# One layer of a vision tower on one core: the front of the kernel rebuilt around a convolution read from PSUM, and the skip term moved to VectorE

## What is computed

```python
h = patches @ proj_w.T + proj_b + pos_emb                 # 1024 tokens x 192
xz = layernorm(h) @ in_proj_w.T                           # 384 channels x, 384 channels gate
x = silu(causal_conv(x, conv_w, K=4) + conv_b)            # per channel, along the 64 tokens of an image
ts, Bm, Cm = split(x @ x_proj_w.T, [48, 64])              # 48, 16, 16
dt = softplus(ts @ dt_proj_w.T + dt_proj_b)               # last token of an image: dt *= alpha
state = exp(A * dt) * state + dt * Bm * x                 # scan along the tokens, 384 x 16 states
y = (sum_n(state * Cm) + x * D) * silu(gate)              # last token: y *= feature_gating
h = h + y @ out_proj_w.T
h = h + shared_ffn(layernorm(h)) + sum of the top 2 of 8 experts, by token
```

## Time and profile before

| | us |
|---|---|
| median of 3 runs | 408.27 (407.31 to 408.51) |
| the profiled execution, its own time | 407.58 |
| its span | 405.5 |
| TensorE busy | 361.1 (89%) |
| VectorE busy | 223.4 (55%) |
| ScalarE busy | 214.6 (53%) |
| GpSimd busy | 218.6 (54%) |

### The profile page before, as it was taken

The page is one execution under the profiler, slowest core; times in us unless marked ns, Lnnn a source line. Parts: engine busy times, 40 slices in busy tenths (PEclk is TensorE's granted clock), DMA queues, the critical chain, the costliest instruction groups (busy, mean ns, idle before and its releaser), DMA issues.

```text
span 405.5 us, 5557 instructions
## 1 busy us (share of the span) xinstructions
PE 361.1 (89%) x1686; PEld 256.8 (63%) x1687; DVE 223.4 (55%) x327; ACT 214.6 (53%) x388; POOL 218.6 (54%) x160
## 2 busy tenths in 40 slices
PE   4798959898997799999999997999999999999970
PEld 3642224554564455566657775778888888888860
DVE  0467849856596284687897466874433232233220
ACT  0045789917599598397458645862333333333310
POOL 2110478967689486488999923770033333443333
PEclk9999969999999899999999958999999999999996
DMA  7950540000004341201059999225223322223211
GB/s 207 309 179 0 224 194 0 0 6 0 2 0 157 154 166 42 78 2 52 2 162 216 240 215 229 82 93 108 66 39 53 60 46 45 45 45 47 40 19 19
DMA packets 28595, 36.95 MB, mean 91 GB/s; under 512 B 6064, under 2 KB 24032, under 8 KB 27552
## 3 DMA queue, kind: packets, MB, share of 16 engines
q1 hardware_dynamic: 18768, 27.38, 24.1%
q0 software_dynamic: 4080, 4.39, 7.0%
q10 hardware_dynamic: 5728, 4.93, 4.3%
HBM read 28.29 MB, written 8.40 MB: 90 GB/s over the span
## 4 chain that ended last, share of the span: by engine, by line
PE 41%; DMA 21%; ACT 12%; DVE 10%; issue 7%; ACTq 5%; POOLq 1%; POOL 1%; SPq 1%; DVEq 0%
DMA out<-ysb,token_r 18%; PE ps L1326 11%; PE ps L1343 5%; ACT decays L710 4%; ACT diagB L698 4%; DVE states L962 4%; PE ps L1481 3%; DMA w_raw<-in_w13T 3%; PE ps L1238 2%; PE ps L1236 2%; ACTq L647 2%; DVE ysb L1142 2%; PE ps L1448 2%; PE ps L1268 1%; PE ps L1247 1%
## 5 line engine op out<-in xcount | busy, mean ns | idle before, releaser
L521 POOL TENSOR_TENSOR states<-states,c_all 128x1024 f32<-128x1024 f32 x48 | 114.2, 2388 | 35.8 <-DVE states L962 35.4
L962 DVE TENSOR_TENSOR_SCAN states<-decays,ps 128x1024 f32<-128x1024 f32 x48 | 109.1, 2282 | 43.8 <-PE ps L1326 34.7
L1326 PE MATMUL ps<-diagB,dt_uT 128*128 128x512 f32 x192 | 94.1, 615 | 1.9 <-ACT dt_uT L688 1.0
L602 POOL DMA_INDIRECT out<-ysb,token_r x23 | 36.1, 1571 | 68.1 <-DVE ysb L1142 62.8
L710 ACT ACTIVATE decays<-dt_uT,negA 128x504 f32<-128x504 f32 x96 | 60.4, 706 | 18.4 <-DVE states L962 18.4
L1343 PEld LDWEIGHTS ps<-ident,states 128*128 128x128 f32 x384 | 44.9, 141 | 22.5 <-issue 21.8
L1326 PEld LDWEIGHTS ps<-diagB,dt_uT 128*128 128x128 f32 x192 | 34.0, 197 | 32.5 <-issue 27.5
L1131 DVE TENSOR_TENSOR hm<-ps,sa 128x512 f32<-128x512 f32 x31 | 21.4, 691 | 55.3 <-PE ps L1454 53.9
L1343 PE MATMUL ps<-ident,states 128*128 128x128 f32 x384 | 49.7, 273 | 0.1
L812 ACT ACTIVATE sa<-ps 128x512 f32<-128x512 f32 x31 | 18.5, 598 | 55.2 <-PE ps L1454 53.8
L1481 PE MATMUL ps<-w,hT 128*128 (+1 forms) x248 | 45.5, 327 | 0.1
(11 more groups left out here) (177 smaller groups left out, 513.7 us busy)
## 6 DMA issues: line engine op xcount, KB each, us to landing
c_all<-c_scratch SPq DMA_DIRECT2D x8, 1024.0 KB, 4.8
w_raw<-in_w13T SPq DMA_DIRECT2D x9, 512.0 KB, 12.6
w_raw<-in_w13T SPq DMA_DIRECT2D x18, 256.0 KB, 12.3
w<-in_w2T SPq DMA_DIRECT2D x9, 384.0 KB, 3.5
xs<-rows_scratch SPq DMA_DIRECT2D x23, 128.0 KB, 2.3
rows_scratch<-dt_uT ACTq DMA_DIRECT2D x5, 520.0 KB, 8.5
c_all<-in_xT SPq DMA_DIRECT2D x4, 256.0 KB, 7.1
c_all<-in_xT SPq DMA_DIRECT2D x1, 1024.0 KB, 12.9
```

What stands on the lines that cost most here:

```text
L521: pool.tensor_tensor(states[:, n % SLOTS, :], states[:, n % SLOTS, :], c_all[:, s, :], ALU.mult).then_inc(cs_ok, 1)
L602: pool.indirect_dma_start(out=out_d, out_offset=bass.IndirectOffsetOnAxis(ap=token_r[:, r:r + 1], axis=0), in_=ysb[:, r, :], in_offset=Non ...
L962: dve.tensor_tensor_scan(states[:, n % SLOTS, :], decays[:, n // PAIRS % DBUF, n % PAIRS, :, :, :].rearrange("p q n s -> p (q n s)"), unit ...
L1326: last = pe.matmul(unit_banks(n)[:, q, :], uT[:, g, i, 128 * t:128 * (t + 1)], diagB[:, s, q, :, :].rearrange("p n t -> p (n t)"), start=T ...
```

## The change

Nothing is computed otherwise; the steps move between engines and in the order.

- The convolution reads the projection in its PSUM bank; `hp`, its zero columns and ScalarE's copies go. The last tap is applied to all tokens first, then the earlier taps to the tokens that have them.
- The seven stores of zeros are issued by SyncE, behind the loads of x, instead of by ScalarE.
- Six patch tiles come before the first transposes (seven before), the last two between the first three projections. VectorE's convolutions of the first half stand between the tiles. The projections 3 to 8 move: 3 behind the first coefficients, 4 to 8 behind the inputs and sums of units 0 to 4. The second half's convolutions follow: (1,0) ahead of scan 0, (1,1) and (1,2) behind scans 0 and 1.
- `dt_softplus` takes a range of chunks: chunk 0 of the first half alone, its decays, then the other two. GpSimd waits for u of chunk 0 after its first pair of diagonals. VectorE instead of ScalarE copies the first transposed u.
- The skip term is a multiply-add on VectorE, in place in PSUM, ahead of the gate's product; `skip` and the matrices `diagD` go. SyncE waits for the gated results instead of the sums.

```diff
+        PATCH_BANK = [0, 1, 4, 5, 0, 1, 0, 1]
@@ sync
+            sp.wait_ge(zero_ok, 1)
+            for z in range(0, SLOT_TILES, 4):
+                end = min(z + 4, SLOT_TILES)
+                sp.dma_start(rows_v[z:end].rearrange("s p d -> p s d"), zeros[:, 0:end - z, :]).then_inc(zero_st, 16)
+            sp.dma_start(sum_v[TT], zeros[:, 0, 0:D]).then_inc(spare_st, 16)
...
-            sp.wait_ge(ysum_mm, IC)
+            sp.wait_ge(y_ok, IC)
@@ gpsimd
             for s in range(POOL_SLICES):
+                if s == 1:
+                    pool.wait_ge(u_ok, 1)
@@ scalar
-            def dt_softplus(g):
-                act.wait_ge(dt_lin, IC * (g + 1))
-                act.preload_act_table_set("natural_log_exp_and_others")
-                chain(act.activation(u[:, :, :], u[:, :, :], ACT.Exp, scale=-1.0))
-                for i in range(IC):
+            def dt_softplus(g, first, end):
+                act.wait_ge(dt_lin, IC * g + end)
+                chain(act.activation(u[:, first:end, :], u[:, first:end, :], ACT.Exp, scale=-1.0))
+                for i in range(first, end):
                     act.activation(u[:, i, :], u[:, i, :], ACT.Ln, bias=1.0).then_inc(lnp_ok, 1)
...
-            act.wait_ge(pads_ok, 1)
+            act.preload_act_table_set("silu_and_others")
             transposed_to_sbuf(act, 0)
-            for n in range(0, IC):
-                projected(n)
-            transposed_to_sbuf(act, 1)
             for i in range(IC):
                 conv_silu(i)
-                projected(IC + i)
-            for i in range(IC):
+            act.preload_act_table_set("natural_log_exp_and_others")
+            transposed_to_sbuf(act, 1)
+            dt_linear(0, 0)
+            dt_softplus(0, 0, 1)
+            act.wait_ge(negA_ok, 1)
+            act.wait_ge(starts_ok, 1)
+            decays_of(0)
+            for i in range(1, IC):
                 dt_linear(0, i)
-            dt_softplus(0)
-
+            decays_of(1)
+            dt_softplus(0, 1, IC)
             act.wait_ge(bt_ok, 1)
             diagonals(0, 5)
...
@@ vector
             summed_rows(0, embedded, h0_ok)
-            summed_rows(1, embedded, h0_ok, (0, 0))
-            normed(1)
+            normed(0)
+            for t in range(TPG, TPG + 2):
+                embedded(t)
+                statistics(t, h0_ok)
...
             def convolved(g, i):
-                dve.wait_ge(hidden_ok, IC * g + i + 1)
+                dve.wait_ge(in_mm, IC * g + i + 1)
+                x = ps[:, PROJ_BANK[IC * g + i], :].rearrange("p (b s) -> p b s", b=GB)
                 out = hid[g][:, i, :].rearrange("p (b s) -> p b s", b=GB)
-                chain(dve.tensor_scalar(out, hp[:, g, i, :, 0:S], par[:, i, P_CW:P_CW + 1],
-                                        par[:, i, P_CB:P_CB + 1], ALU.mult, ALU.add))
-                for k in range(1, K):
-                    ins = dve.scalar_tensor_tensor(out, hp[:, g, i, :, k:k + S], par[:, i, P_CW + k:P_CW + k + 1],
-                                                   out, ALU.mult, ALU.add)
+                chain(dve.tensor_scalar(out, x, par[:, i, P_CW + K - 1:P_CW + K], par[:, i, P_CB:P_CB + 1],
+                                        ALU.mult, ALU.add))
+                for back in range(1, K):
+                    tap = P_CW + K - 1 - back
+                    ins = dve.scalar_tensor_tensor(out[:, :, back:], x[:, :, 0:S - back], par[:, i, tap:tap + 1],
+                                                   out[:, :, back:], ALU.mult, ALU.add)
...
-            for i in range(IC):
-                convolved(0, i)
-            convolved(1, 0)
+            convolved(0, 0)
+            embedded(TPG + 2)
+            statistics(TPG + 2, h0_ok)
+            convolved(0, 1)
+            embedded(TPG + 3)
+            moments(1, h0_ok)
+            convolved(0, 2)
+            normed(1)
             scan_coefficients(0)
-            convolved(1, 1)
             b_columns(0)
-            convolved(1, 2)
-            dve.wait_ge(conv_ok, IC * G)
@@ gated_sum
+                dve.scalar_tensor_tensor(ps[:, YBANK, :], hid[g][:, i, :], par[:, i, P_D:P_D + 1], ps[:, YBANK, :],
+                                         ALU.mult, ALU.add).then_inc(skip_ok, 1)
+                dve.wait_ge(skip_ok, z + 1)
                 dve.tensor_tensor(sg[:, g, i, :], ps[:, YBANK, :], sg[:, g, i, :], ALU.mult).then_inc(y_ok, 1)
@@ the loop of VectorE
             time_step(0, 0)
+            dve.wait_ge(uT_mm, 1)
+            dve.tensor_copy(uT[:, 0, 0, :], ps[:, YBANK, :]).then_inc(uT_ok, 1)
+            convolved(1, 0)
             for n in range(UNITS):
                 scanned(n)
+                if n < 2:
+                    convolved(1, n + 1)
@@ tensor
+            CONVOLVED = {4: 1, 5: 2, 6: 6, 7: 3, 8: 4}
 
             def project(n):
                 g, m = ORDER[n]
-                if n in PROJ_FREE:
-                    pe.wait_ge(hidden_ok, PROJ_FREE[n])
+                if n < 2:
+                    pe.wait_ge(h0_ok, n + 3)
+                if n in CONVOLVED:
+                    pe.wait_ge(conv_ok, CONVOLVED[n])
+                if n == 7:
+                    pe.wait_ge(uT_ok, 1)
+                if n > 9:
+                    pe.wait_ge(hidden_ok, n - 2 * IC)
...
+            pe.wait_ge(ld_proj, 16)
+            for t in range(TPG + 2):
+                embed(t)
+            pe.wait_ge(ident_ok, 2)
+            transposes(0)
             pe.wait_ge(xnT_ok, 2)
             pe.wait_ge(ld_par, 48)
-            for n in range(IC):
-                project(n)
-            transposes(1)
-            pe.wait_ge(xnT_ok, 2 * G)
-            for n in range(IC, 2 * IC):
-                project(n)
+            project(0)
+            embed(TPG + 2)
+            project(1)
+            embed(TPG + 3)
+            project(2)
             pe.wait_ge(ld_mid, 80)
             pe.wait_ge(h0_ok, TT)
-            coefficients(0)
-            project(2 * IC)
             for i in range(IC):
-                time_step_product(0, i)
+                coefficient_part(0, i)
+            transposes(1)
+            time_step_product(0, 0)
             b_transposes(0)
-            for n in range(2 * IC + 1, 3 * IC):
-                project(n)
-            pe.wait_ge(diag_ok, IC)
+            pe.wait_ge(xnT_ok, 2 * G)
+            project(IC)
             u_transposes(0, 0)
+            time_step_product(0, 1)
+            time_step_product(0, 2)
...
                     pe.wait_ge(bt_ok, 1)
+                    pe.wait_ge(dt_lin, 1)
+                if n == 1:
                     pe.wait_ge(dt_lin, IC)
...
-            def skip(z):
-
-                g, i = z // IC, z % IC
+            def time_order(z):
+
                 if z:
                     pe.wait_ge(y_ok, z)
                 else:
-                    pe.wait_ge(hidden_ok, 2 * IC + 2)
+                    pe.wait_ge(hidden_ok, 2)
                 if z == G * IC - 1:
                     pe.wait_ge(x_low_ok, 2)
-                pe.matmul(ps[:, YBANK, :], diagD[:, i, :], hid[g][:, i, :], start=True, stop=True)
-
-            def sum_after_skip(z):
                 pe.wait_ge(yT_ok, z + 1)
                 for q in range(TPG):
-                    last = pe.matmul(ps[:, YBANK, 128 * q:128 * (q + 1)], yT(z)[:, 128 * q:128 * (q + 1)], ident[:, :],
-                                     start=False, stop=True, is_transpose=True, skip_group_check=True)
+                    last = pe.transpose(ps[:, YBANK, 128 * q:128 * (q + 1)], yT(z)[:, 128 * q:128 * (q + 1)], ident[:, :])
                 last.then_inc(ysum_mm, 1)
...
+                if n < 5:
+                    project(IC + 1 + n)
```

More of the change, by code:

```diff
@@ L475, in _ @@
                 load_half(v)
-            sp.wait_ge(ysum_mm, G * IC)
+            sp.wait_ge(y_ok, G * IC)
             load_half(17)
@@ L642, in _ @@
             act.dma_start(gateTb[:, :], gateT_d[DA:D, :]).then_inc(ld_mid, 16)
-            act.wait_ge(zero_ok, 1)
-            for z in range(0, SLOT_TILES, 4):
-                end = min(z + 4, SLOT_TILES)
-                act.dma_start(rows_v[z:end].rearrange("s p d -> p s d"), zeros[:, 0:end - z, :]).then_inc(zero_st, 16)
-            act.dma_start(sum_v[TT], zeros[:, 0, 0:D]).then_inc(spare_st, 16)
             def conv_silu(i):
@@ L867, in moments, with summed_rows @@
                 last.then_inc(aggr_ok, 1)
-            def summed_rows(g, add, added, last_norm=None):
+            def summed_rows(g, add, added):
                 tiles = range(TPG * g, TPG * (g + 1))
@@ L876, in summed_rows @@
                         statistics(t - 1, added)
-                    if last_norm and t == tiles[last_norm[1]]:
-                        normed(last_norm[0])
                 moments(g, added)
@@ L1212, in last_transposes, with embed @@
                 last.then_inc(xn_tr, 1)
-            pe.wait_ge(ld_proj, 16)
-            for t in range(TT):
+            def embed(t):
                 if t <= TPG:
```

(37 more changed lines are left out.)

53 lines of the change are left out of this document (18 added, 35 removed).

## The result

The changed kernel takes 412.66 us (median of 20 runs) against 408.82 for the kernel before (20 runs beside it). The ratio is 1.0088, with a 95% interval of 1.0066 to 1.0111: it is 0.9% slower, where 403.8 was predicted. Medians here are over all executions of a kernel; a ratio leaves out those that are over 1.5% above the fastest of their kernel (two of the 20 here, 455.43 and 920.92). The other 18 lie between 409.83 and 414.89. The profiled one took 414.06 us, near the upper end, and its span is 412.3.

What follows compares the result with a forecast made beforehand. Bound: the front's dependence chain, then TensorE in full scan stretches. Front -3.5, skip term -0.86, -0.6, +0.45, sum -4.5 from 407.58: 403.1; with 0.7 for the median, 403.8 us, range 401 to 408.

Steps and rivals of the forecast that it cites:

- two rivals: TensorE's clock falls ahead of the coefficients' last third (chance 0.12), or once ahead of projection 6 (chance 0.16).
- the fall ahead of the last third: Rival: clock falls in the 31.6 to 34.3 wait, stays 1.2 GHz until scan 0; 6.7 us, total 410.5; chance 0.12.
- the one ahead of projection 6: Rival: TensorE's clock falls once in the 2.9 us gap there; 2.3 us lost, total 406.1; chance 0.16.
- the walk: Step-by-step timing of the changed front, with scan 0 at 46.1 and scan 8 at 81.2; 401 to 405.3, chance 0.54.
- Zero stores at nothing, projection 0 at 20.75: Front's start: SP issues the zero stores at no cost; projection 0 starts at 20.75, 2.15 us earlier.
- Convolution from PSUM 3.0: VectorE's convolution straight from PSUM: 0.67 plus 2.33, 3.0 us a chunk, with bounds 2.8 and 5.0.
- Not slowed by the diagonals: PSUM multiply-adds keep their speed beside GpSimd's diagonals; rival, 1.4 each, 2.7 us lost, 406.5, chance 0.10.
- Scan 0 at 46.1: End of the front: first scan starts at 46.1 us instead of 60.24, 14.1 earlier.
- the wait ahead of projection 6 at 2.9: Among the first scans: TensorE idles from about 53.9 to 56.8, until VectorE's sixth convolution is done.
- scan 8 at 81.2: After the moved projections: scan 8 starts at 81.2 against 84.75, so the front gives 3.5 us.
- From unit 8 to 157 nothing in the order changes that is on the path: Middle scans: skip products of z=0 and z=1 lie in waits, so the front's 3.5 us pass through.
- The skip term: x * D moved to VectorE: 0.86 us gained at z=2, 0.6 at z=3, nothing at z=4, 0.45 lost at z=5.

Runs made afterwards that it cites:

- before_filled: Kernel before with five thrown-away products in TensorE's wait for the first u: 413.76 us, ratio 0.9994.
- zeros_alone: Kernel before with only the seven stores of zeros moved from ScalarE to SyncE, behind the loads of x: 407.62 us, ratio 0.9984.
- skip_undone: Changed kernel with the skip term back on TensorE: 405.78 us once, 413.55 to 414.96 three times, no total given.
- five_skip_on_tensor: Changed kernel with thrown-away products in four front waits (x, last third, behind projection 3, ahead of projection 6) and skip term on TensorE: 404.69 us, ratio 0.9912.
- projections_trimmed: `projections_filled` with one thrown-away product each at units 12 and 20, two behind unit 2's inputs, instead of three: 400.56 us, ratio 0.9837.
- skip_alone: Kernel before with only the skip term moved to VectorE: 407.29 us, ratio 0.9975.
- fill_five: Changed kernel with thrown-away products in five waits: x, last third, behind projection 3, ahead of projection 6, unit 12: 404.07 us, ratio 0.9881.
- fill_second: Changed kernel with three thrown-away products in TensorE's wait ahead of projection 6 only: 411.58 us, ratio 1.0034.
- fill_by_projections: Changed kernel with projection 4 behind 3, 5 behind unit 0's inputs, 6 to 8 behind units 3 to 5: 403.17 us, ratio 0.9874.
- projections_filled: `fill_by_projections` plus thrown-away products in waits for x, the last third, behind unit 2's inputs, at units 12 and 20: 401.50 us, ratio 0.9831.

## Why the prediction was wrong

**The step that failed** is that TensorE's clock stays at 2.4 GHz through the new waits of the front. It stood in the text as two rivals, with chances of 0.12 and 0.16, each by itself. Both came true, and they add. A third fall, at unit 12, had no price at all. The prediction's prices were 6.7 us for the fall ahead of the last third and 2.3 for the one ahead of projection 6; 403.8 + 9.0 is 412.8, and 412.66 was measured. That the two agree so closely is partly luck, since both prices were off and more was lost elsewhere. In the profiled execution the first cost 5.9 (scan 0 at 51.98 against the walk's 46.1) and the second 3.2 (38.3 us from scan 0 to scan 8 instead of 35.1); the third cost 1.6. The rival's reason for a long fall, that TensorE is busy only in pieces, doesn't hold: it was busy for 16.00 of 16 us.

The chance was mis-set by the evidence. One row, 2.22 us of idle with the clock still at 1.00, was taken as evidence against a fall in the new waits, and shorter waits were not looked at. The same waits, one profiled execution of each kernel, show what it is worth:

| wait | idle us, clock stayed | idle us, clock fell |
|---|---|---|
| last load of x (1.4 or more) | nine, 1.40 to 2.22 | three, 2.15 to 2.84 |
| last third of the coefficients | two, 2.48 and 2.49 | four, 2.49 |
| behind projection 3 | none | three, 1.88 |
| ahead of projection 6 | none | four, 2.68 to 2.90 |
| unit 12, without the skip product | three, 1.93 and 1.94 | four, 1.93 and 1.94 |

Both outcomes occur for waits of one length, at one and the same line. The second error is one of reckoning: two rivals of one mechanism are not independent, and a range that ends at 408 leaves out each sum with the larger one in it.

**Step by step**, the terms of the sum:
- Zero stores at nothing, projection 0 at 20.75: right (20.46, with x there at 15.55).
- Convolution from PSUM 3.0: right, 3.07. The Trainium skill, "VectorE: DVE Perf Modes", Rules for kernel authors, names a copy to SBUF first as the way for many operations. Here the multiply-adds from PSUM (2.27 for 504, 496 and 488 columns) are about as fast as those from SBUF (2.33 for three of 512). Only the first operation is slower, 0.80 against 0.54 in the kernel before, so that a copy, which took ScalarE 0.6, would not pay.

```profile
27.19 0.54 DVE L923 TENSOR_SCALAR hidden<-states,par 128x512 f32<-128x512 f32 x1
```

- Not slowed by the diagonals: right, 2.27 beside them.
- Scan 0 at 46.1, the wait ahead of projection 6 at 2.9, scan 8 at 81.2: right where the clock stays up (45.93, 2.68 in the changed kernel, 80.86). The front is worth 3.5 to 3.9 us.
- "From unit 8 to 157 nothing in the order changes that is on the path: the skip product of z=0 and z=1 lies in waits for ScalarE's copy": wrong in what it leaves out. The product cost no time, but it kept TensorE busy in that wait. Without it the clock fell at unit 12 in four of seven profiled executions, for 1.6 us in the changed kernel's; with one product in the wait (the kernel before, `before_filled`, `zeros_alone`, `skip_undone`, `five_skip_on_tensor`, `projections_trimmed`) it fell in none of six. That VectorE's multiply-add is hidden there was right: with the skip term alone scan 8 is 0.40 late, from the front, and scan 28 0.48.
- The skip term: predicted 0.86 for z=2, 0.6 for z=3, nothing for z=4, -0.45 at the end. In the changed kernel it is 0.85 (scan 29), 0.33 (scan 37), 0.85 (scan 47) and -0.43. z=4 was mis-sized. The load of the weights that the prediction puts last starts behind a product of GpSimd that follows the scans, so it comes earlier with them: in `skip_alone` at 210.06 and not at 211.04. In the changed kernel it isn't on the chain there. The parts come to 1.6 and not 1.0; that `skip_alone` is 1.0 faster in all is partly luck. In its profile the parts come to 1.55 (0.89, 0.35, 0.86, less 0.55), of which 0.48 are lost ahead of scan 28 and 0.67 behind the first expert product.
- From the first expert product on, the profiled execution is 1.5 us longer than before, which no step had. The median is 1.4 below that execution, and the other profiles lie between -0.5 and +1.4 there, but for `fill_five` with +6.8; it may be the spread of executions, which was not tested.

**Where 11.0 us went** (403.1 forecast for the execution, 414.06 measured): 9.1 the two falls, 1.6 the third, 1.5 the tail, less 0.8 in the scans behind unit 13 and 0.3 around the span (1.76 against 2.08), which is 11.1, the rest rounding.

What stays open: what decides in an execution whether such a wait makes the clock fall, and how long it then stays down. By the runs it is not the order of the program alone.

## What to carry to other kernels

A rebuild that takes work out of the front of a chain of dependences opens waits on TensorE, and the waits must be priced with the clock: behind each, the work may take twice its time until the clock is back. Before moving products away from a place where TensorE waits, look at whether they are what keeps it busy there; real work put into such waits (the projections here) made the kernel 1.3% faster than the one before instead of 0.9% slower, and with fillers besides 1.6% to 1.7%. A filler must not be longer than the wait: three took back 0.7 us where one took nothing. If two rivals share a mechanism, forecast them together, and do not take one row that shows no effect for a bound.

## What the runs showed of the hardware

**The half clock can last through full work.** In the changed kernel it stayed at 0.50 for 17 us, with TensorE busy for all of the 16 us from 36 to 52, and so it did in `fill_second` and `skip_undone`. In `fill_by_projections`, behind the same wait and over the same instructions, it was back after 3.4 us:

```profile
36.00:38.00 2.00, 1.64 (x5) 0.90 (x6) 1.04 (x4) 1.59 (x2) 0.00 (x0) 0.77 0.03 8
38.00:40.00 2.00, 2.00 (x8) 1.34 (x7) 0.45 (x1) 0.54 (x2) 0.00 (x0) 0.50 0.04 9
40.00:42.00 2.00, 2.00 (x8) 0.62 (x6) 0.22 (x1) 1.46 (x4) 0.28 (x1) 0.88 0.03 7
```

The Trainium skill, "TensorE: Matmul & The Clock Gate", Part 1: The HAM clock gate, has the full clock return once TensorE is kept busy for a while; by that rule the first fall would have cost what it cost in `fill_by_projections`, and not 5.9: there scan 0 started at 50.11, 3.7 behind `projections_filled` (46.41), of which 2.1 were lost before projection 0, so 1.6. The trace of the changed kernel does not agree.

**In one execution the clock also fell without a wait.** In `before_filled` TensorE was busy from 40 to 60 us, and still:

```profile
40.00:44.00 4.00, 4.00 (x11) 1.53 (x10) 2.99 (x5) 0.32 (x1) 0.00 (x0) 1.00 0.04 8
44.00:48.00 4.00, 4.00 (x11) 1.46 (x10) 2.53 (x5) 3.98 (x7) 1.88 (x2) 0.69 0.73 254
48.00:52.00 4.00, 4.00 (x5) 0.99 (x5) 3.93 (x3) 3.96 (x7) 4.00 (x4) 0.50 1.00 418
52.00:56.00 4.00, 4.00 (x5) 1.39 (x6) 2.65 (x3) 2.09 (x8) 4.00 (x4) 0.50 0.89 377
```

It is one execution, 6.1 us above the kernel's profile without fillers, and no other profile shows the like up to 125 us. It says only that waits may not be the one cause.
